# A Fourier-domain block MLP on one Trainium2 core: the first unit's weights are loaded from ScalarE's queue and readied later, and a unit's unfolding begins two groups later

## The chip, the cores and the metric

The kernel runs on one core of one Trainium2 chip. The metric is the device time of an execution in microseconds (us). The time before is a median of three executions; beside it stands one profiled execution, from which all rows below are taken.

## The reference

The input x has shape (4, 128, 128, 768), float32. Everything is computed in float32.

```
xf = rfft2(x, axes=(1, 2), norm='ortho')             # 128 x 65 frequencies, 8 blocks of 96 channels
o1r = relu(xr @ w1[0] - xi @ w1[1] + b1[0]);  o1i = relu(xi @ w1[0] + xr @ w1[1] + b1[1])
o2r = o1r @ w2[0] - o1i @ w2[1] + b2[0];      o2i = o1i @ w2[0] + o1r @ w2[1] + b2[1]
o = softshrink(o2, 0.01)                             # per real and imaginary part
out = irfft2(o, s=(128, 128), norm='ortho') + x
```

## The kernel before

**Units and stages.** A unit is one image with one block of 96 channels, so there are 4 x 8 = 32 units, two by two in the buffers `xs[0]` and `xs[1]` (`par` is the buffer, `m` the pair, `n` the unit). For each unit TensorE runs stage A (DFT along one axis, 24 steps of four rows), then the *layers*, then the *inverse* (stages E and F). The layers go over 17 groups of frequencies (`NS` = 17), `s` running from 0 to 18 because three stages are in flight at once: stage B (first matmul), stage C (DFT along the other axis, which is where the ReLU comes), stage D (second matmul). In the inverse, stage E is the inverse DFT along one axis and stage F the one along the other, in 24 chunks.

**Order of TensorE.** Stage A of unit 0 alone; then for every unit: layers, the first two steps of stage A of the next unit, inverse, the other 22 steps of stage A of the next unit, the last two chunks of F. The engines are separate programs that meet in semaphores; nothing reorders them at run time. The loop holds four units; the first unit's layers of TensorE's loop body and the inverse in the bodies of ScalarE and VectorE are where their programs branch back.

**x in and out.** x is loaded in four pieces, by 50 transfers a unit (14 + 12 + 12 + 12). Before stage A the rows are *folded* (sum and difference of mirrored rows). GpSimd does that for all units but the first (`fold`), which VectorE folds at the start of its program (L578 to L590). Before it folds the next unit, GpSimd multiplies a third of the current unit's x by a half (`halve`, L458), as soon as VectorE has set `first_halved` (L663, the end of `forward`). After the inverse VectorE *unfolds* the unit's x, which has become the result: eight steps, `unfold_step`, one in each of the groups s = 0 to 7 of the next unit's layers. Each odd step releases a piece (`unfolded`), and SyncE then stores that piece, and loads the same piece of the unit two further on. After the first piece's stores SyncE also issues the 28 loads of the next weights for that buffer (`load_w`).

**Weights.** `prepare_step` k = 0 to 8 on VectorE readies the weights of a unit: k = 0 waits until all 28 transfers have landed and negates a part of w1, k = 1 negates another, k = 2 to 5 negate parts of w2 (together they set `w_negated`, which stage B of group 0 waits for), k = 6 to 8 split the second bias (`b2_split`, which stage D of group 0 waits for). They stand in the groups s = 8 to 16 of the layers of the unit before; the first unit's nine stand ahead of `forward(0)`.

**Evictions of stage A.** ScalarE and VectorE take turns in copying the steps of stage A from PSUM (`forward`). TensorE's step 6 needs ScalarE's second copy and step 7 VectorE's second copy.

**SyncE at the start.** The DFT matrices, the 50 transfers of unit 0's x, the 28 of its weights, the 50 of unit 1's x, its 28 of weights.

Of the kernel before, what the change touches and what calls it, by code (L numbers as in the profile page):

```python
# [12 lines left out]
IMAGES, SIZE, HIDDEN, BLOCKS = 4, 128, 768, 8  # L13
BLOCK = HIDDEN // BLOCKS
UNITS = IMAGES * BLOCKS
HALF = SIZE // 2
# [40 lines left out]
NP = len(PIECES)  # L57
# [40 lines left out]
def sum_rows(b):  # L98
# [4 lines left out]
    if b == 0:  # L103
# [14 lines left out]
SEGMENTS = [(0, 0, BLOCK, 0, 0), (0, BLOCK, SIZE, 1, 0), (1, 0, HALF, 1, SIZE - BLOCK), (1, HALF, SIZE, 0, 0),  # L118
            (2, 0, BLOCK - HALF, 0, HALF), (2, BLOCK - HALF, SIZE, 1, 0)]

W2_COLUMNS = [tile * 2 * BLOCK for tile, *_ in SEGMENTS]
# [38 lines left out]
def fourier_mlp(nc, x, w1, b1, w2, b2, dft, out):  # L160
    with ExitStack() as ctx:
# [35 lines left out]
        w1_whole = [sb(f"w1_whole{i}", [SIZE, 2, BLOCK]) for i in range(2)]  # L197
# [158 lines left out]
        def evict_views(g):  # L356
# [5 lines left out]
                return U[0:BLOCK, own:own + A_ROWS - 1, j:j + SIZE], U[0:BLOCK, HALF:HALF + 1, 2:SIZE + 2], third  # L362
            return U[0:BLOCK, own:own + A_ROWS, j:j + SIZE], third

        @block.sync
        def _(sp):
            def load_piece(m, par, p):
                for tile, image in transfers(xs[par], pixels(x, m, par), p):
                    sp.dma_start(tile, image).then_inc(x_loaded[par][p], 16)  # L369

            def load_w(m, par):
                blk = (m % PER_IMAGE) * 2 + par

                def put(dst, src):
                    sp.dma_start(dst, src).then_inc(w_loaded[par], 16)

                put(w1_whole[par][0:BLOCK], w1[:, blk].rearrange("r i o -> i r o"))
                for t, lo, rows in ((w1_whole, BLOCK, slice(HALF, BLOCK)), (w1_halved, 0, slice(0, HALF)),
                                    (w1_halved, HALF, slice(0, HALF))):
                    for half in range(2):  # L380
                        put(t[par][lo:lo + rows.stop - rows.start, half], w1[half ^ 1, blk, rows])
                for (tile, lo, hi, r, c), col in zip(SEGMENTS, W2_COLUMNS):
                    rows = slice(c, c + hi - lo)
                    for half in range(2):

                        put(w2t[par][lo:hi, col + half * BLOCK:col + (half + 1) * BLOCK], w2[half ^ r, blk, rows])
                    with nc.allow_non_contiguous_dma(reason="a bias on each partition"):
                        put(b1t[par][lo:hi, tile:tile + 1], b1[r, blk, rows].unsqueeze(1))
                put(b2_rows[par][:, :, :], b2[:, blk].partition_broadcast(SIZE))
                for row in (0, LOW_ROW):  # L390
                    put(b2t[par][row:row + 1, :].rearrange("p (r c) -> p r c", r=2), b2[:, blk].unsqueeze(0))

            def store_piece(m, par, p):
                sp.wait_ge(unfolded, (m * 2 + par) * NP + (p + 1))
                for tile, image in transfers(xs[par], pixels(out, m, par), p):
                    sp.dma_start(image, tile).then_inc(x_stored[par][p], 16)

            sp.dma_start(mats[:, :], dft[:, 0:7 * SIZE]).then_inc(mats_loaded, 16)
            sp.dma_start(excess[:, :, :].rearrange("p a b -> p (a b)")[:, 0:2 * SIZE],
                         dft[:, 7 * SIZE:]).then_inc(iw_loaded, 16)  # L400
            for p in range(NP):
                load_piece(0, 0, p)
            load_w(0, 0)
            for p in range(NP):
                load_piece(0, 1, p)
            load_w(0, 1)
            with sp.Fori(0, PAIRS - 1) as m:
                for par in range(2):

                    for p in range(NP + 1):  # L410
                        if p < NP:
                            store_piece(m, par, p)
                        if p > 0:
                            sp.wait_ge(x_stored[par][p - 1], (m + 1) * (16 * TRANSFERS[p - 1]))
                            load_piece(m + 1, par, p - 1)
                        if p == 0:
                            load_w(m + 1, par)
            for par in range(2):
                for p in range(NP):
                    store_piece(PAIRS - 1, par, p)  # L420
            for par in range(2):
                for p in range(NP):
                    sp.wait_ge(x_stored[par][p], PAIRS * (16 * TRANSFERS[p]))
# [50 lines left out]
        def _(act):  # L474
# [28 lines left out]
            def forward(n):  # L503
                for at in A_ACT:
                    act.wait_ge(a_done, n * NA + (at + 1))
                    src = bank_a(at).rearrange("p (s j) -> p s j", s=A_ROWS)
                    rows, third = evict_views(A_ORDER[at])
                    act.activation(rows, src[0:BLOCK], ACT.Copy)
                    act.activation(third, src[BLOCK:], ACT.Copy).then_inc(act_copied, 1)
# [38 lines left out]
            def body(loop, unit, last=False):  # L548
# [3 lines left out]
                forward(n)  # L552
                layers(m, par, n)

            forward(0)
            layers(0, 0, 0)
            with act.Fori(0, PAIRS // UNROLL - 1) as loop:
# [7 lines left out]
        def _(dve):  # L565
# [28 lines left out]
            def unfold_step(n, par, k):  # L594

                x_unit, (lo, hi) = xs[par], PIECES[k // 2]
                up, down = x_unit[:, lo:hi + 1, :], mirrored(x_unit, lo, hi)
                if k == 0:
                    dve.wait_ge(f_added, n * NF + NF)
                    dve.wait_ge(f_late_added, n * LATE + LATE)  # L600

                even, odd = x_unit[:, 0, BLOCK:], x_unit[:, MIDDLE, BLOCK:]
                if k % 2 == 0:
                    if k == 0:
                        dve.tensor_tensor(even, even, odd, ALU.add)
                    dve.tensor_tensor(up, up, down, ALU.add).then_inc(unfold_even, 1)
                else:
                    dve.wait_ge(unfold_even, n * NP + (k // 2 + 1))
                    if k == 1:
                        dve.scalar_tensor_tensor(odd, odd, -2.0, even, op0=ALU.mult, op1=ALU.add)  # L610
                    dve.scalar_tensor_tensor(down, down, -2.0, up, op0=ALU.mult, op1=ALU.add).then_inc(unfolded, 1)
# [52 lines left out]
            def layers(m, par, n, first, last):  # L664
                for s in range(NS + 2):
                    if s < NS:
                        k = pairs(s)
                        dve.wait_ge(b_done, n * NS + (s + 1))
                        dve.tensor_copy(mixed[s % 2][:, 0:k], both_b(s)[:, 0:k]).then_inc(b_copied, 1)  # L669
                    for stage in ("sums", "tiles") if s < NS else ("tiles", "sums"):  # L670
                        if stage == "sums" and s >= 2:
                            t, rows = s - 2, rows_d(s - 2)
                            j = 2 + 2 * GROUPS[t][0]
                            dst = real_kw[:, :, :] if t == REAL else U[:, 0:BLOCK, j:j + rows]
                            dve.wait_ge(excess_done, n * NS + (t + 1))
                            dve.scalar_tensor_tensor(dst, parts_d(t), LAMBDA, excess[:, :, 0:rows], op0=ALU.add,  # L676
                                                     op1=ALU.min).then_inc(shrunk, 1)
                        if stage == "tiles" and 1 <= s <= NS:
                            t = s - 1
                            dve.wait_ge(c_done, n * NS + (t + 1))  # L680
                            dve.tensor_scalar(middle[t % 2][:, 0:pairs(t)], middle_c[:, 0:pairs(t)], b1t[par][:, 1:2], 0.0,
                                              ALU.add, ALU.max).then_inc(middle_done, 1)
                    if 2 <= s < NS:

                        k = rows_d(s) // 2
                        dve.wait_ge(shrunk, n * NS + (s - 1))
                        dve.tensor_copy(bank_d(s).rearrange("p (k r) c -> p k r c", r=2)[:, 0:k],  # L687
                                        b2_rows[par][:, :, :].unsqueeze(1).broadcast_to([SIZE, k, 2, BLOCK])).then_inc(seeded, 1)

                    if s < 2 * NP and not first:  # L690
                        unfold_step(n - 1, 1 - par, s)

                    if 2 * NP <= s < 2 * NP + PREPARE and not last:
                        prepare_step(m + par, 1 - par, s - 2 * NP)
            def add(par, n, q):

                x_unit = xs[par]
# [30 lines left out]
                layers(m, par, n, False, last)  # L728


            for k in range(PREPARE):
                prepare_step(0, 0, k)
            forward(0)
            layers(0, 0, 0, True, False)
            with dve.Fori(0, PAIRS // UNROLL - 1) as loop:
                for unit in range(2 * UNROLL):
# [210 lines left out]
```

## Time and profile before

| | us |
|---|---|
| median of 3 executions | 5112.62 (5111.63 to 5113.49) |
| profiled execution, its own time | 5110.49 |
| its span, first to last instruction | 5108.7 |
| TensorE busy | 4994.3 (98%) |
| VectorE busy | 3881.6 (76%) |
| ScalarE busy | 2996.4 (59%) |
| GpSimd busy | 1437.3 (28%) |
| mean granted TensorE clock | 0.994 |

A granted clock of 1.0 is 2.4 GHz and one of 0.5 is 1.2 GHz. PE is TensorE's matmuls, PEld its weight loads, DVE VectorE, ACT ScalarE, POOL GpSimd, SPq SyncE's queue. A float32 matmul of the code is two in the trace. Times in the trace count from the span's start. Stage B of unit 0 begins at 72.48 us, and an undisturbed unit takes 156.56 us from there to the next.

### The profile page before, as it was taken

What the parts mean: (1) busy time and instruction counts of PE and PEld (TensorE: products, weight loads), DVE (VectorE), ACT (ScalarE), POOL (GpSimd) and SP (SyncE); (2) the same over time, 40 slices, a digit from 0 to 9 for tenths busy, and PEclk for the clock granted to TensorE, in tenths of its full rate; (3) what the DMA queues carried; (4) which work ended last, traced back from release to release, by engine and by line L of the source; (5) the groups of instructions that cost most, each with busy time, mean ns of one, the idle gap of its engine ahead of it and who ended that gap; (6) DMA issues with size and microseconds to landing.
All of it is one profiled execution on the core that took longest, in us unless ns stands there. A gap on an engine that the chain in (4) does not pass through costs nothing.

```text
span 5108.7 us, 113601 instructions
## 1 busy us (share of the span) xinstructions
PE 4994.3 (98%) x40128; PEld 4694.0 (92%) x40128; DVE 3881.6 (76%) x6163; ACT 2996.4 (59%) x5409; POOL 1437.3 (28%) x905
## 2 busy tenths in 40 slices
PE   6999999999999999999999999999999999999997
PEld 5999999999999999999999999999999999999996
DVE  4777778777777777777778777788777787777885
ACT  4555665556655566555566555665556655556653
POOL 3033222333123332233331233312333223333120
PEclk8999999999999999999999999999999999999998
DMA  5044422344323444234443234432344422344332
GB/s 113 16 90 105 105 66 57 88 105 105 82 58 83 93 105 102 56 68 90 105 105 68 61 82 105 105 85 62 77 92 105 105 57 65 89 105 105 80 68 57
DMA packets 1699974, 430.34 MB, mean 84 GB/s; under 512 B 1699104, under 2 KB 1699232, under 8 KB 1699360
## 3 DMA queue, kind: packets, MB, share of 16 engines
q1 hardware_dynamic: 1699360, 422.47, 37.4%
q8 instruction: 346, 5.67, 0.5%
q14 instruction: 268, 2.20, 0.1%
HBM read 220.89 MB, written 201.33 MB: 83 GB/s over the span
## 4 chain that ended last, share of the span: by engine, by line
PE 96%; DVE 2%; SPq 1%; issue 1%; ACT 0%; DMA 0%; ACTq 0%; DVEq 0%
PE psum L816 15%; PE psum L787 14%; PE psum L769 13%; PE psum L866 13%; PE psum L839 13%; PE psum L849 9%; PE psum L799 7%; PE psum L876 3%; PE psum L877 3%; PE psum L878 3%; DVE mixed L669 1%; SPq L369 1%; DVE spectrum L647 0%; PE psum L834 0%; PE psum L857 0%
## 5 line engine op out<-in xcount | busy, mean ns | idle before, releaser
L669 DVE COPY mixed<-psum 128x768 f32<-128x768 f32 (+1 forms) x544 | 507.8, 933 | 707.0 <-PE psum L799 705.2
L546 ACT ACTIVATE sums_high<-psum 128x512 fp32r<-128x512 f32 x768 | 459.6, 599 | 730.9 <-PE psum L866 730.9
L816 PEld LDWEIGHTS psum<-mats,mixed 128*128 128x128 f32 x6272 | 744.0, 191 | 121.2 <-issue 113.0
L816 PE MATMUL psum<-mats,mixed 128*128 128x128 f32 x6272 | 841.8, 283 | 0.0
L787 PE MATMUL psum<-w_whole,whole 128*128 128x192 f32 x4160 | 779.3, 329 | 33.0 <-ACT whole L487 13.3
L839 PE MATMUL psum<-w2t,hidden 128*128 128x192 f32 x4160 | 768.2, 327 | 0.0
L769 PE MATMUL psum<-mats,x 128*128 128x128 f32 x6144 | 704.7, 277 | 44.6 <-DVE spectrum L647 28.8
L866 PE MATMUL psum<-mats,spectrum 128*128 128x128 f32 x6144 | 745.1, 275 | 1.7 <-DVE spectrum L676 1.7
L769 PEld LDWEIGHTS psum<-mats,x 128*128 128x128 f32 x6144 | 696.0, 193 | 51.7 <-DVE spectrum L647 29.0
L710 DVE TENSOR_TENSOR sums_low<-psum,sums_high 128x512 fp32r<-128x512 f32 x768 | 531.2, 692 | 247.6 <-ACT sums_high L546 247.3
L787 PEld LDWEIGHTS psum<-w_whole,whole 128*128 128x128 f32 x4160 | 670.9, 196 | 52.2 <-issue 22.9
L866 PEld LDWEIGHTS psum<-mats,spectrum 128*128 128x128 f32 x6144 | 716.2, 192 | 2.4 <-DVE spectrum L676 1.9
L529 ACT ACTIVATE excess<-psum,over 128x768 f32<-128x768 f32 (+1 forms) x544 | 481.8, 886 | 370.3 <-PE psum L849 367.9
L839 PEld LDWEIGHTS psum<-w2t,hidden 128*128 128x128 f32 x4160 | 688.1, 190 | 7.2 <-issue 7.2
L458 POOL TENSOR_TENSOR x<-x,half 128x3072 f32<-128x3072 f32 x32 | 169.8, 5307 | 1730.8 <-DVE halved L663 1730.8
L535 ACT ACTIVATE hidden<-psum,b1t 128x256 f32<-128x256 f32 (+1 forms) x544 | 254.6, 468 | 666.8 <-PE psum L816 666.8
L676 DVE SCALAR_TENSOR_TENSOR spectrum<-psum,excess 128x768 f32<-128x768 f32 (+1 forms) x512 | 481.0, 940 | 109.0 <-ACT excess L529 104.1
L849 PE MATMUL psum<-w2t,middle 64*128 64x192 f32 x4160 | 490.3, 350 | 0.0
L876 PE MATMUL psum<-sums_high,iw_high 128*128 128x260 f32 (+1 forms) x1536 | 461.8, 301 | 0.0
L687 DVE COPY psum<-b_rows 128x768 f32<-128x768 f32 (+1 forms) x480 | 449.9, 937 | 0.0
L450 POOL TENSOR_TENSOR x<-x,doubled 128x640 f32<-128x640 f32 (+1 forms) x248 | 442.7, 1785 | 17.0
L445 POOL TENSOR_TENSOR x<-x 128x640 f32<-128x640 f32 (+1 forms) x248 | 443.8, 1790 | 0.0
(83 smaller groups left out, 7526.3 us busy)
## 6 DMA issues: line engine op xcount, KB each, us to landing
x<-x SPq DMA_DIRECT2D x736, 192.0 KB, 2.9
out<-x SPq DMA_DIRECT2D x736, 192.0 KB, 2.5
x<-x SPq DMA_DIRECT2D x736, 64.0 KB, 2.6
out<-x SPq DMA_DIRECT2D x736, 64.0 KB, 2.2
x<-x SPq DMA_DIRECT2D x32, 144.0 KB, 2.6
w2t<-L_conv_w SPq DMA_DIRECT2D x128, 36.0 KB
out<-x SPq DMA_DIRECT2D x32, 144.0 KB, 2.3
x<-x SPq DMA_DIRECT2D x64, 48.0 KB, 2.3
```

Of the source, the lines that this page charges most:

```text
L529: act.activation(excess[:, :, 0:rows_d(t)], parts_d(t), ACT.Relu, bias=over[:, 0:1]).then_inc(excess_done, 1)
L546: act.activation(sums_high[:, q % RING], bank_e(q), ACT.Copy).then_inc(high_copied, 1)
L669: dve.tensor_copy(mixed[s % 2][:, 0:k], both_b(s)[:, 0:k]).then_inc(b_copied, 1)
L676: dve.scalar_tensor_tensor(dst, parts_d(t), LAMBDA, excess[:, :, 0:rows], op0=ALU.add, op1=ALU.min).then_inc(shrunk, 1)
L710: dve.tensor_tensor(sums_low[:, q % RING], bank_e(q), sums_high[:, q % RING], ALU.subtract).then_inc(low_copied, 1)
L769: last = pe.matmul(bank_a(at)[:, i * SIZE:(i + 1) * SIZE], xs[par][:, j, :], mat(FW_EVEN if g[0] < NP else FW_ODD), start=True, stop=True)
L787: pe.matmul(bank_b(s, k), whole[s % 2][:, k // 2, :, k % 2], w1_whole[par][:, :, :].rearrange("p r o -> p (r o)"), start=k % 2 == 0, stop= ...
L816: last = pe.matmul(out[tile], flat[:, tile * SIZE:(tile + 1) * SIZE], mat(FH), start=True, stop=True)
L839: pe.matmul(sums_d(s, k), hidden[s % 2][:, k // 2, k % 2], w2_tile(par, slice(0, SIZE), 2 * (k // 2)), start=False, stop=False, skip_group ...
L849: last = pe.matmul(sums_d(s, i + 2 * y), middle[s % 2][rows, i], w2_tile(par, rows, 1), start=False, stop=True, skip_group_check=True)
L866: last = pe.matmul(bank_e(q)[:, :, i], U[:, q * CHUNK + i, 4:], mat(IH_FIRST if q * CHUNK < THIRD else IH), start=True, stop=True)
L876: pe.matmul(out, iw_high[:, j], high, start=True, stop=False)
```

## The change

`load_w` becomes a function that takes the engine. The first unit's 28 weight transfers are issued from ScalarE's queue, at the head of its program, and no longer from SyncE's between the two units' x. On VectorE `forward(0)` goes ahead of the first unit's nine `prepare_step`s. In the layers the unfolding stands in the groups 2 to 9 and the preparing in 10 to 18, where they stood in 0 to 7 and 8 to 16.

```diff
+        def load_w(engine, m, par):              # body as before, with engine.dma_start
         @block.sync
...
             for p in range(NP):
                 load_piece(0, 0, p)
-            load_w(0, 0)
             for p in range(NP):
                 load_piece(0, 1, p)
-            load_w(0, 1)
+            load_w(sp, 0, 1)
...
         @block.scalar
+            load_w(act, 0, 0)
             forward(0)
             layers(0, 0, 0)
...
         @block.vector
-                    if s < 2 * NP and not first:
-                        unfold_step(n - 1, 1 - par, s)
-                    if 2 * NP <= s < 2 * NP + PREPARE and not last:
-                        prepare_step(m + par, 1 - par, s - 2 * NP)
+                    if 2 <= s < 2 + 2 * NP and not first:
+                        unfold_step(n - 1, 1 - par, s - 2)
+                    if 2 + 2 * NP <= s < 2 + 2 * NP + PREPARE and not last:
+                        prepare_step(m + par, 1 - par, s - 2 - 2 * NP)
...
+            forward(0)
             for k in range(PREPARE):
                 prepare_step(0, 0, k)
-            forward(0)
             layers(0, 0, 0, True, False)
```

## Rows read from the trace of the kernel before

**Rows 1.** Waits of TensorE, whole span: us in total, times, longest.
```profile
PE psum L769 <- DVE spectrum L647: 28.8, 1, 28.8
...
PE psum L787 <- ACT whole L487: 13.3, 26, 1.9
PE psum L787 <- ACT whole L480: 11.3, 6, 2.1
...
PE psum L866 <- DVE spectrum L676: 1.7, 1, 1.7
```
**Rows 2.** Timeline of the start: start, length, instruction, idle before.
```profile
1.67 28.95 SPq L369 DMA_DIRECT2D x<-x  x50
...
36.41 0.16 DVE L592 MEMSET spectrum<- 96x126 f32 x1
...
45.15 1.36 SPq L375 DMA_DIRECT2D b2t<-L_conv_b  x2
...
47.80 0.21 DVE L620 TENSOR_SCALAR w_whole<-w_whole 32x96 f32<-32x96 f32 x1 [11.23 <-DMA b2t<-L_conv_b]
...
48.28 0.91 DVE L624 TENSOR_SCALAR w2t<-w2t 32x96 f32<-32x96 f32 x4
...
50.22 0.17 DVE L637 MEMSET spectrum<- 96x130 f32 x1
...
53.18 17.38 PE L769 MATMUL psum<-mats,x 128*128 128x128 f32 x136 [28.84 <-DVE spectrum L647]
```
**Rows 3.** Windows: length, busy (count) per engine, granted clock, DMA share, GB/s.
```profile
12.00:31.00 19.00, 8.60 (x58) 8.43 (x58) 10.60 (x9) 4.75 (x8) 0.00 (x0) 0.88 1.03 234
...
249.00:266.00 17.00, 17.00 (x138) 15.67 (x134) 14.22 (x15) 11.62 (x22) 0.00 (x0) 1.00 0.19 36
...
53.20:57.20 4.00, 4.00 (x19) 4.00 (x20) 2.71 (x4) 0.20 (x1) 0.00 (x0) 0.50 0.90 190
57.30:70.50 13.20, 13.20 (x119) 13.06 (x117) 10.10 (x20) 9.34 (x17) 0.00 (x0) 1.00 1.01 210
```
**Rows 4.** Timeline, end of unit 0's stage A and begin of its layers.
```profile
72.48 1.58 PE L787 MATMUL psum<-w_whole,whole 128*128 128x192 f32 x8 [1.92 <-ACT whole L487]
72.57 0.22 DVE L663 COPY halved<-spectrum 64x66 f32<-64x66 f32 x1
72.94 5.31 POOL L458 TENSOR_TENSOR x<-x,half 128x3072 f32<-128x3072 f32 x1 [72.10 <-DVE halved L663]
...
80.29 1.54 POOL L445 TENSOR_TENSOR x<-x 128x640 f32<-128x640 f32 x1
```
**Rows 5.** Timeline, VectorE instructions that overlap one of GpSimd in unit 1.
```profile
229.44 5.31 POOL L458 TENSOR_TENSOR x<-x,half 128x3072 f32<-128x3072 f32 x1 [109.01 <-DVE halved L663]
...
232.40 2.40 DVE L605 TENSOR_TENSOR x<-x 128x32 f32<-128x32 f32 x1
...
308.75 1.82 POOL L450 TENSOR_TENSOR x<-x,doubled 128x768 f32<-128x768 f32 x1
308.99 1.70 DVE L626 CAST b_parts<-b2t 1x192 fp32r<-1x192 f32 x1
```
**Rows 6.** Windows of the same columns: unit 0 (no unfolding), unit 1 (unfolding).
```profile
72.40:228.90 156.50, 155.87 (x1254) 146.50 (x1254) 100.92 (x178) 93.45 (x171) 46.12 (x29) 1.00 0.06 12
229.00:385.50 156.50, 155.86 (x1254) 146.50 (x1254) 120.11 (x193) 93.51 (x170) 46.11 (x29) 1.00 0.39 86
```
**Rows 7.** Timeline of unit 1: unfolding, store, the last fold stretch, the layers' end.
```profile
239.20 9.06 SPq L396 DMA_DIRECT2D out<-x  x14
...
246.57 1.75 DVE L611 SCALAR_TENSOR_TENSOR x<-x 128x1536 f32<-128x1536 f32 x1
...
315.04 1.47 POOL L444 TENSOR_TENSOR doubled<-x 128x768 f32<-128x768 f32 x1 [4.47 <-DMA x<-x]
...
325.80 0.76 DVE L676 SCALAR_TENSOR_TENSOR spectrum<-psum,excess 128x576 f32<-128x576 f32 x1 [0.92 <-ACT excess L529]
...
326.99 3.74 PE L866 MATMUL psum<-mats,spectrum 128*128 128x128 f32 x32
```

More of the change, by code:

```diff
@@ L363, in evict_views, with put @@
             return U[0:BLOCK, own:own + A_ROWS, j:j + SIZE], third
+        def load_w(engine, m, par):
+            blk = (m % PER_IMAGE) * 2 + par
+            def put(dst, src):
+                engine.dma_start(dst, src).then_inc(w_loaded[par], 16)
+            put(w1_whole[par][0:BLOCK], w1[:, blk].rearrange("r i o -> i r o"))
+            for t, lo, rows in ((w1_whole, BLOCK, slice(HALF, BLOCK)), (w1_halved, 0, slice(0, HALF)),
+                                (w1_halved, HALF, slice(0, HALF))):
+                for half in range(2):
+                    put(t[par][lo:lo + rows.stop - rows.start, half], w1[half ^ 1, blk, rows])
+            for (tile, lo, hi, r, c), col in zip(SEGMENTS, W2_COLUMNS):
+                rows = slice(c, c + hi - lo)
+                for half in range(2):
+                    put(w2t[par][lo:hi, col + half * BLOCK:col + (half + 1) * BLOCK], w2[half ^ r, blk, rows])
+                with nc.allow_non_contiguous_dma(reason="a bias on each partition"):
+                    put(b1t[par][lo:hi, tile:tile + 1], b1[r, blk, rows].unsqueeze(1))
+            put(b2_rows[par][:, :, :], b2[:, blk].partition_broadcast(SIZE))
+            for row in (0, LOW_ROW):
+                put(b2t[par][row:row + 1, :].rearrange("p (r c) -> p r c", r=2), b2[:, blk].unsqueeze(0))
         @block.sync
@@ L369, in load_piece @@
                     sp.dma_start(tile, image).then_inc(x_loaded[par][p], 16)
[L371 to L391, printed above, removed]
             def store_piece(m, par, p):
@@ L416, in _ @@
                         if p == 0:
-                            load_w(m + 1, par)
+                            load_w(sp, m + 1, par)
             for par in range(2):
```

## The prediction

> **What bounds the kernel now.** The busy table says 98% for TensorE, so I read its waits first, then the places where they stand. Over the whole span TensorE waits for little: once 28.8 us in the first unit's stage A for VectorE's copies, 13.3 us in 26 units for ScalarE's first gather, 11.3 us in six units for a later gather (only where the loop branches back), and once for VectorE's last shrink [rows 1]. The only large stall is the first. The timeline of the start shows what is behind it: VectorE has done its last folding and its memset at 36.41 + 0.16 = 36.57, then stands idle for 11.23 us until the last weight transfer lands, readies the weights in nine short steps from 47.80, and comes to the first instruction of `forward(0)` at 50.22; TensorE, which needs the second copy of that function, goes on at 53.18 [rows 2]. The weights are late because their 28 issues stand in SyncE's queue behind 50 of x, which take until 1.67 + 28.95 = 30.62 [rows 2].
>
> The windows of unit 0 and unit 1 answer the other half. Unit 0 has no unfolding and unit 1 has it; in 156.50 us TensorE has 1254 matmuls and 155.87 and 155.86 us of busy time [rows 6]. VectorE's 19 us more of work cost TensorE nothing, so moving the unfolding to other groups has nothing to win; it can only lose.
>
> **The first stall.** With the wait for the weights gone from ahead of `forward(0)`, its first instruction follows at 36.57 and no longer at 50.22: **-13.65 us**, if x lands when it did. ScalarE's 28 issues last about what SyncE's did, 45.15 + 1.36 - 30.62 = 15.9 us [rows 2], so ScalarE is free for its evictions near 18 us; its first four are wanted only when VectorE's second is there, around 40. That is cover of 20 us, and it costs nothing. SyncE's queue, freed of the 28, brings unit 1's x and weights some 13 us earlier; nobody waits for them yet.
>
> The weights now share the 16 DMA engines with x. In unit 1 the same 28 transfers are alone in the queue and take 0.19 of 17.0 us, 3.2 us of all engines [rows 3]. From 12 to 31 us the share under x alone is 1.03 [rows 3], so there is no room and the last piece of x lands later by the weights' work: **+3.0 us**. The bounds are 0 (the work fits into gaps) and 15.9 (every issue of ScalarE holds up one of SyncE); I stay near the row of the work, as the engines are what is full.
>
> On the last point the Trainium skill has a rule. Perfetto Trace Analysis, in its section on the HWDGE DMA instruction, draws one descriptor generator that two sequencers share, with a wait for its lock. By it the term would be up to 15.9 us and not 3.0. No row here has two queues issuing at once.
>
> **What the nine steps cost in their new place.** They stand between `forward(0)` and the layers now, and stage B of group 0 waits for the first six. At their old speed these take 48.28 + 0.91 - 47.80 = 1.39 us [rows 2]; after L663, which ends at 72.79, that would put stage B at 74.2 where it was 72.48 [rows 4] (I keep the clock of before for this part; all of it comes earlier together). But L663 also releases GpSimd's halving, 5.31 us from 72.94 [rows 4], and the two engines exclude one another in such operations. L605, a 32-element operation, took 2.40 us and ended when GpSimd's L458 did (229.44 + 5.31 = 234.75); L626, on one partition, took 1.70 us and ended with GpSimd's L450 [rows 5]. So: step 0 slips in and ends at 73.03; the halving runs to 78.34; step 1 follows; GpSimd now goes on to fold unit 1, whose x has landed by then, and steps 2 to 5 each get in between two of its four short operations, which fill the 2.04 us from the halving's end at 78.25 to L445 at 80.29 [rows 4]. The sixth step ends near 80.4 and stage B begins near 80.5: **+8.0 us**. The lower bound is 1.8 (the six go through in one burst), the upper 10 (each meets a long fold step). Steps 6 to 8 lie beside stage B of group 0, and cost nothing.
>
> TensorE is then idle for 10 us from 70.56 (53.18 + 17.38). After its long wait the granted clock was 0.50 from 53.2 to 57.2, and 19 matmuls were done where 13.20 us at 1.00 have 119 [rows 2, 3]: 210 ns each for 111. I count such a stretch once more: 4.0 x (1 - 111/210) = **+1.9 us**.
>
> Start in all: -13.65 + 3.0 + 8.0 + 1.9 = -0.75 us.
>
> **The move by two groups.** The unfolding's second step, which releases the first store at 239.20, now ends where the fourth did: 246.57 + 1.75 less the first piece's smaller size, 248.3. SyncE is busy without a break from there, so stores, loads, and GpSimd's folding are all 9.4 us later. Folding ends near 315.04 + 20 + 9.4 = 345. Its last piece feeds the last six steps of stage A, 48 matmuls at 111 ns and two chunks of F ahead of unit 2's stage B at 385.6 (229.04 + 156.56), so about 378: cover of 30 us remains. Unfolding ends before folding starts, as before.
>
> Preparing now reaches into the end of the layers. Step 7 stands ahead of VectorE's last shrink, L676 at 325.80, which had 0.92 us of idle time before it and ends 326.99 - 326.56 = 0.43 us before stage E begins [rows 7]. Free of GpSimd, step 7 fits (such a step takes 0.21 us [rows 2]). GpSimd's last unbroken stretch of folding, from 315.04 for 20 us [rows 7], is moved to 324.5, so that it is busy just then in nearly every unit. If step 7 has to wait w for a fold operation and ends with it, as L626 did, TensorE loses w - 0.92 - 0.43 = w - 1.35 us. The fold operations are one of 1.47 and two of 1.82 us in turn [rows 5, 7]; over an arbitrary phase that is (2 x 0.47^2 / 2 + 0.12^2 / 2) / 5.11 = 0.045 us a unit, in 30 units **+1.3 us**. The bounds are 0 (step 7 always falls right) and 0.47 x 30 = 14 (the phase always falls worst). Step 8 comes after the last shrink, with 2 us to the next work of VectorE.
>
> In six units the programs of VectorE and ScalarE branch back just as stage E begins, and the x loads, now 9 to 11 us later, reach into that moment. What the wait for a branch costs beside loads has no row; the nearest is the 11.3 us in six units where TensorE branches [rows 1]. Bounds 0 and 11; I take **+1 us**, since an idle DMA queue did not spare TensorE that wait either.
>
> **Sum.** -0.75 + 1.3 + 1.0 = +1.55 us on the profiled execution's 5110.49, that is 5112.0. The median of the runs, 5112.62, lies 2.1 us above the profiled execution, so 5114.2 for the median. 0.2% of it, 10.2 us, is what a measurement can tell from no change: below 5102.4 is faster, above 5122.8 slower.
>
> **The rivals.**
> *The steps go through in one burst.* For it: the nine ran without a gap when GpSimd was idle [rows 2]. Against it: both rows of an overlap show VectorE wait for GpSimd's whole operation [rows 5]. The sum has 1.8 for 8.0: 5108.0; with nothing for DMA work, clock and move, 5100.8, the only way to the faster side. Chance 0.25. The Trainium skill, SBUF - State Buffer, "Who interferes with whom", says that whichever starts first has the shared ports for its whole instruction; by it this rival is out and the 8.0 stands.
>
> *The issues of the two queues wait for each other.* Then each of ScalarE's 28 puts SyncE's back, the last x lands 15.9 us later, and the stall is not shorter but 2.3 us longer: 5114.2 + 12.9 = 5127.1, slower. It decides from a delay of x of 11.6 us on (3.0 and the 8.6 up to 5122.8). For it: an issue of either kind takes about 0.57 us, whatever its bytes (28.95/50, 15.9/28 [rows 2]), so it isn't the data that sets it. Against it: the DMA share of 1.03 says the engines are the limit. Chance 0.11.
>
> *The phase locks at the worst.* Step 7 meets the begin of a long fold operation in most units: up to 12.7 us more, 5127, slower. Landing times vary by some us between units, which speaks against it. Chance 0.06.
>
> My forecast has the remaining 0.58. Faster gets 0.08, from the first rival's far end; slower gets 0.14, mostly the second and third; the same 0.78. The range reaches from the first rival's lower middle, 5104, to 5122.
>
> **What would show it.** Stage B of unit 0 should begin near 70 us (72.48 - 10.65 + 8.0), with a wait of 10 us ahead of it and VectorE's L620 on `w1_halved` over 5 us long beside L458. TensorE's first wait should be 18 us for 28.8. The last x of unit 0 should land about 3 us later. The stretch from unit to unit should stay 156.56 us in most units, with single ones 0.1 to 0.6 us longer and a wait of E on L676. If stage B of unit 0 begins at 64, the lock was wrong; if above 80, the queues block each other.

## The result, and the profile after

The changed kernel takes 5119.27 us (median of 11 runs) where the kernel before takes 5111.61 (11 runs beside it): ratio 1.0018, 95% interval 1.0010 to 1.0026, so 7.7 us more by the medians; the interval is 0.10 to 0.26%. The forecast was 5114.2, which is +1.6 us on its own base. The direction and the range hold; four fifths of the size were not in the sum. Of all runs here and below one counts as slow and is left out of its ratio: 5677 us, in the experiment in which GpSimd waits. The profiled execution's span is 5116.5 us against 5108.7, +7.8, nearly the difference of the medians, so that its rows can be added up.

First the waits of TensorE in the changed kernel, over the whole span (us in total, times, longest); lines have moved by one against [rows 1].

```profile
PE psum L770 <- DVE x L591: 17.5, 2, 16.5
PE psum L770 <- DVE spectrum L648: 15.8, 1, 15.8
PE psum L788 <- ACT whole L486: 11.4, 25, 0.6
PE psum L788 <- ACT whole L479: 11.3, 6, 2.2
PE psum L788 <- DVE w2t L625: 10.2, 1, 10.2
...
PE psum L867 <- DVE sums_low L711: 2.4, 4, 1.2
PE psum L867 <- DVE spectrum L677: 1.7, 1, 1.7
```

The reader is to see three things. The wait of 28.8 us is now 15.8; of these 13.0 us the start gained only 11.2, as the waits for the first folded pieces of x (L591, 17.5 us where they were 15.7 before, a wait that the prediction did not list) grew by 1.8. A wait of 10.2 us for L625, the negating of w2, has come. And stage E (L867) waits for VectorE's low sums, four times, which it never did for more than 0.1 us before (the view counts no wait under 0.15 us; two more of 0.11 and 0.12 are there).

The timeline of the start, to be held against [rows 2] and [rows 4]:

```profile
1.66 61.20 SPq L391 DMA_DIRECT2D x<-x  x100
...
15.04 1.82 ACTq L369 DMA_DIRECT2D b2t<-L_conv_b  x2
...
35.28 1.76 DVE L587 TENSOR_TENSOR x<-x 128x1536 f32<-128x1536 f32 x1 [3.21 <-DMA x<-x]
...
39.01 0.17 DVE L638 MEMSET spectrum<- 96x130 f32 x1
...
41.97 17.96 PE L770 MATMUL psum<-mats,x 128*128 128x128 f32 x136 [15.84 <-DVE spectrum L648]
...
61.95 0.22 DVE L664 COPY halved<-spectrum 64x66 f32<-64x66 f32 x1
62.20 0.21 DVE L621 TENSOR_SCALAR w_whole<-w_whole 32x96 f32<-32x96 f32 x1
62.32 5.30 POOL L457 TENSOR_TENSOR x<-x,half 128x3072 f32<-128x3072 f32 x1 [61.48 <-DVE halved L664]
...
62.44 5.25 DVE L621 TENSOR_SCALAR w_halved<-w_halved 128x96 f32<-128x96 f32 x1
...
67.72 2.08 DVE L625 TENSOR_SCALAR w2t<-w2t 32x96 f32<-32x96 f32 x4
...
70.13 2.92 PE L788 MATMUL psum<-w_whole,whole 128*128 128x192 f32 x8 [10.20 <-DVE w2t L625]
```

`forward(0)` begins at 39.01 for 50.22, 11.2 us earlier. Stage A ends 10.6 us earlier (41.97 + 17.96 = 59.93 for 70.56). Stage B begins 2.35 us earlier (70.13 for 72.48): 8.3 us are lost between these two. The second L621, on `w_halved`, takes 0.21 us when alone (in the run in which GpSimd waits, below) and here ends with GpSimd's L457.

Windows around stage B of unit 0, and around the begin of unit 16 (columns as in [rows 3]):

```profile
70.20:74.50 4.30, 4.30 (x16) 3.49 (x16) 3.01 (x3) 0.00 (x0) 4.14 (x4) 0.50 0.12 25
74.60:80.00 5.40, 5.40 (x38) 4.96 (x37) 2.00 (x3) 4.60 (x9) 5.18 (x5) 1.00 0.24 32
...
2586.80:2590.10 3.30, 3.30 (x15) 2.42 (x14) 0.08 (x1) 0.08 (x1) 3.30 (x1) 0.50 0.00 0
2590.20:2594.00 3.80, 3.80 (x28) 3.36 (x27) 1.82 (x3) 2.97 (x7) 0.00 (x0) 1.00 0.00 0
```

The first line of each pair is a stretch at 0.50 of the clock. After the first of them unit 1's stage B begins at 228.76, where it was at 229.04: at that point all that the start gives is 0.28 us.

```profile
228.76 0.93 PE L788 MATMUL psum<-w_whole,whole 128*128 128x192 f32 x4 [0.43 <-ACT whole L486]
```

The rest of the time is read from the distances of the stage-B begins from unit to unit, after less before:

| where | us |
|---|---|
| begin of unit 0's stage B | -2.35 |
| unit 0 | +2.07 |
| the six units in which VectorE and ScalarE branch back (4, 8, ... 24) | +6.63 |
| the six units that end in TensorE's branch | +0.15 |
| the other 18 | +1.02 |
| the last | +0.32 |

Together that is 7.8 us, the difference of the spans. So the layers of an ordinary unit cost nearly nothing, and the six branching units carry the loss. Here is the worst, unit 8, at the begin of its stage E, first in the changed kernel:

```profile
1423.28 1.82 POOL L444 TENSOR_TENSOR x<-x 128x768 f32<-128x768 f32 x1
1423.91 1.31 DVE L629 CAST b_high<-b2t 1x192 fp32r<-1x192 f32 x1
...
1425.25 0.76 DVE L677 SCALAR_TENSOR_TENSOR spectrum<-psum,excess 128x576 f32<-128x576 f32 x1
...
1426.04 1.17 DVE L632 TENSOR_TENSOR b_parts<-b2t,b_high 1x192 fp32r<-1x192 f32 x1
...
1429.50 1.89 DVE L711 TENSOR_TENSOR sums_low<-psum,sums_high 128x512 fp32r<-128x512 f32 x3 [2.29 <-ACT sums_high L545]
1430.25 0.94 PE L867 MATMUL psum<-mats,spectrum 128*128 128x128 f32 x6 [1.24 <-DVE sums_low L711]
```

and in the kernel before:

```profile
1424.71 0.76 DVE L676 SCALAR_TENSOR_TENSOR spectrum<-psum,excess 128x576 f32<-128x576 f32 x1 [0.92 <-ACT excess L529]
...
1427.98 1.29 DVE L710 TENSOR_TENSOR sums_low<-psum,sums_high 128x512 fp32r<-128x512 f32 x2 [2.51 <-ACT sums_high L546]
```

After the last shrink VectorE needs 2.51 us to its first low sum in the kernel before, though ScalarE's high sum, which the column names, was there at 1427.60: in between lies the branch back of VectorE's program. In the changed kernel it is 3.49 us from the end of the shrink (1426.01 to 1429.50), and TensorE, whose fourth chunk of stage E waits for it, stands for 1.24 us. Two things are new in the place: L632 of the preparing, lengthened by GpSimd, and x in the queues (GpSimd is busy for 5.84 of 6 us in both). The windows from 1424 to 1430, before and after (the columns as above, the last two the DMA share and GB/s):

```profile
1424.00:1430.00 6.00, 6.00 (x53) 5.83 (x53) 2.63 (x4) 2.95 (x6) 5.84 (x5) 1.00 0.03 8
```

```profile
1424.00:1430.00 6.00, 5.00 (x42) 4.69 (x42) 3.64 (x4) 2.96 (x5) 5.84 (x4) 1.00 0.83 164
```

Which of the two delays VectorE was the question of the first experiments.

### The profile page after: what moved, and what is told of

Its sections match the earlier page's. It is cut to its first block, busy times and chain, and to the rows that moved or that the text cites. A ratio compares the mean times of both kernels' runs of the same rounds, so it can differ in the third digit from the quotient of the medians.

```text
span 5116.5 us, 113601 instructions
## 1 busy us (share of the span) xinstructions
PE 5002.0 (98%) x40128; PEld 4698.7 (92%) x40128; DVE 3828.6 (75%) x6163; ACT 2995.7 (59%) x5409; POOL 1437.1 (28%) x905
## 4 chain that ended last, share of the span: by engine, by line
PE 95%; DVE 2%; issue 1%; SPq 1%; ACT 0%; DMA 0%; DVEq 0%; ACTq 0%
PE psum L817 15%; PE psum L788 14%; PE psum L770 13%; PE psum L840 13%; PE psum L867 13%; PE psum L850 9%; PE psum L800 7%; PE psum L877 3%; PE psum L878 3%; PE psum L879 3%; DVE mixed L670 1%; SPq L391 1%; DVE spectrum L648 0%; PE psum L835 0%; PE psum L858 0%
## 5 line engine op out<-in xcount | busy, mean ns | idle before, releaser
L867 PE MATMUL psum<-mats,spectrum 128*128 128x128 f32 x6144 | 746.8, 275 | 4.4 <-DVE sums_low L711 2.4
L770 PE MATMUL psum<-mats,x 128*128 128x128 f32 x6144 | 705.5, 277 | 33.3 <-DVE x L591 17.5
L867 PEld LDWEIGHTS psum<-mats,spectrum 128*128 128x128 f32 x6144 | 716.2, 192 | 6.6 <-DVE sums_low L711 3.8
L457 POOL TENSOR_TENSOR x<-x,half 128x3072 f32<-128x3072 f32 x32 | 169.8, 5306 | 1428.0 <-DVE halved L664 1428.0
L440 POOL TENSOR_TENSOR x<-x 128x192 f32<-128x192 f32 x31 | 15.7, 506 | 1739.3 <-DMA x<-x 1739.3
```

The source lines that it names most:

```text
L770: last = pe.matmul(bank_a(at)[:, i * SIZE:(i + 1) * SIZE], xs[par][:, j, :], mat(FW_EVEN if g[0] < NP else FW_ODD), start=True, stop=True)
L867: last = pe.matmul(bank_e(q)[:, :, i], U[:, q * CHUNK + i, 4:], mat(IH_FIRST if q * CHUNK < THIRD else IH), start=True, stop=True)
```

## The experiments

Each was run beside the kernel before on the same chip. The ratios are to it, with their 95% intervals; a difference in us is of the medians.

**The two halves of the change.** First the start alone (layers as before):

```diff
-                    if 2 <= s < 2 + 2 * NP and not first:
-                        unfold_step(n - 1, 1 - par, s - 2)
+                    if s < 2 * NP and not first:
+                        unfold_step(n - 1, 1 - par, s)
...
-                    if 2 + 2 * NP <= s < 2 + 2 * NP + PREPARE and not last:
-                        prepare_step(m + par, 1 - par, s - 2 - 2 * NP)
+                    if 2 * NP <= s < 2 * NP + PREPARE and not last:
+                        prepare_step(m + par, 1 - par, s - 2 * NP)
```

> Only the start of the change: ScalarE issues the first weights, the nine steps stand behind the first stage A; the layers are as before. My theory (the start wins 13 us of waiting and gives it all back to GpSimd's halving and a low clock): stage B of unit 0 again near 70.1 us with a 10 us wait ahead of it, the time within 1.5 us of before (-0.3 us by the profile of the changed kernel), and every later unit as before. Rival (the start itself costs what was measured, by a clock or DMA effect that lasts): +4 us or more.

Measured: 5110.80 against 5111.40, ratio 0.9999 (0.9990 to 1.0008). The waits:

```profile
PE psum L770 <- DVE spectrum L648: 15.6, 1, 15.6
...
PE psum L788 <- DVE w2t L625: 10.2, 1, 10.2
```

The start is worth -0.6 us, and 0 lies within the interval. My theory holds; no effect of it that lasts is seen.

Then the move by two groups alone, put into the kernel before (the same lines the other way round, and nothing else).

> Only the move by two groups, unfolding in groups 2 to 9 and preparing in 10 to 18; the start is as before. My theory: it carries the whole loss, +7 to +8.5 us. Waits of stage E on VectorE's low sums in the six units where the programs branch back, 2 to 4 us in all, and about 1.3 us of late last shrinks. Rival: the loss sits in the start, and this run is within 2 us of before.

Measured: 5122.30 against 5111.40, ratio 1.0020 (1.0011 to 1.0029), +10.9 us, more than I expected; its interval overlaps that of the whole change nearly in full. The move carries the loss.

```profile
PE psum L866 <- DVE sums_low L710: 4.1, 6, 1.1
PE psum L866 <- DVE spectrum L676: 3.0, 7, 1.6
```

The second row holds the last unit's 1.6 us, which every kernel here has; the other 1.4 us are six late last shrinks.

**The two halves of the move.** Preparing alone in groups 10 to 18, with unfolding, stores and loads where they were:

```diff
-                    if 2 * NP <= s < 2 * NP + PREPARE and not last:
-                        prepare_step(m + par, 1 - par, s - 2 * NP)
+                    if 2 + 2 * NP <= s < 2 + 2 * NP + PREPARE and not last:
+                        prepare_step(m + par, 1 - par, s - 2 - 2 * NP)
```

> Unfolding in groups 0 to 7 as before, so stores, loads and GpSimd's folding at their old times; only preparing moved to groups 10 to 18. Theory A (preparing's last two steps, which wait for GpSimd's fold operations, stand ahead of the last shrink and ahead of VectorE's branch): the loss is here without any load beside it, +3 to +6 us, VectorE's first low sum 1 us or more late in the branching units. Theory B (the x loads, moved into the moment of the branch, slow the fetch of the programs): the branching units are as before, the run is at +1.5 us at most, from the late shrinks alone.

Measured: 5115.73 against 5111.40, ratio 1.0010 (1.0001 to 1.0019), +4.3 us.

```profile
PE psum L866 <- DVE spectrum L676: 3.1, 6, 1.7
PE psum L866 <- DVE sums_low L710: 0.5, 2, 0.2
```

The time is as theory A says, but not where it says it: the low sums are waited for only twice, 0.5 us in all (and three times for 0.10 to 0.15 us, which the view leaves out). In unit 8 of this run the first low sum starts 1.15 us after L631 ends (1428.53 + 1.17 = 1429.70 to 1430.85), 2.35 us after the end of the shrink, which is less than before (2.51). So VectorE's branch does not wait for step 8 in full. What is late is the last shrink, behind step 7; stage E begins later for it in eleven units, by 0.67 us at most. In unit 8 (L628 is step 7, L631 step 8) the shrink follows step 7 at once, though ScalarE's part of it had been there for 0.43 us:

```profile
1426.45 1.26 DVE L628 CAST b_high<-b2t 1x192 fp32r<-1x192 f32 x1
1427.74 0.76 DVE L676 SCALAR_TENSOR_TENSOR spectrum<-psum,excess 128x576 f32<-128x576 f32 x1
1428.53 1.17 DVE L631 TENSOR_TENSOR b_parts<-b2t,b_high 1x192 fp32r<-1x192 f32 x1
1430.85 2.01 DVE L710 TENSOR_TENSOR sums_low<-psum,sums_high 128x512 fp32r<-128x512 f32 x3 [1.15 <-ACT sums_high L546]
```

Then the unfolding two groups later, so with the loads at their new times, but the preparing packed so that none of it is left for the groups 17 and 18:

```diff
-                    if s < 2 * NP and not first:
-                        unfold_step(n - 1, 1 - par, s)
+                    if 2 <= s < 2 + 2 * NP and not first:
+                        unfold_step(n - 1, 1 - par, s - 2)
...
-                    if 2 * NP <= s < 2 * NP + PREPARE and not last:
-                        prepare_step(m + par, 1 - par, s - 2 * NP)
+                    if 2 + 2 * NP <= s < NS and not last:
+                        lo = (0, 2)[s - 2 - 2 * NP] if s - 2 - 2 * NP < 2 else s - 2 * NP
+                        for k in range(lo, lo + (2 if s - 2 - 2 * NP < 2 else 1)):
+                            prepare_step(m + par, 1 - par, k)
```

> Unfolding in groups 2 to 9, loads 9.4 us later as in the change; the nine preparing steps packed into groups 10 to 16 (two in each of the first two), so that none is left for groups 17 and 18. Theory A (the last two preparing steps): within 1 us of before, no wait of stage E beyond 0.1 us. Theory B (the loads beside the branch): +3 to +6 us, with VectorE's first low sum late in the branching units though nothing stands ahead of the branch.

Measured: 5115.41 against 5111.40, ratio 1.0008 (0.9999 to 1.0017), +4.0 us, as theory B says.

```profile
PE psum L868 <- DVE sums_low L712: 3.2, 6, 1.1
PE psum L868 <- DVE spectrum L676: 1.7, 1, 1.7
```

No late shrink is left beside the last unit's, and the waits for low sums are all there, in all six branching units. In unit 8:

```profile
1424.24 0.76 DVE L676 SCALAR_TENSOR_TENSOR spectrum<-psum,excess 128x576 f32<-128x576 f32 x1 [0.92 <-ACT excess L529]
1428.45 1.89 DVE L712 TENSOR_TENSOR sums_low<-psum,sums_high 128x512 fp32r<-128x512 f32 x3 [3.45 <-ACT sums_high L546]
```

3.45 us from the shrink to the first low sum with nothing between them but the branch, where it was 2.51; the DMA share of the moment is 0.78 (1423.50 to 1429.50) and was 0.03. In the six branching units this distance is 2.72 to 3.61 us and was 2.27 to 2.59. That a program is fetched there can be seen in the DMA queues. From 1424.80 to 1428.00 of the kernel before they carry four packets of the kind `instruction` and nothing else; in this run, from 1424.30 to 1428.50 (packets, MB, share of the engines):

```profile
q1 hardware_dynamic: 3069, 0.75, 86.4%
q14 instruction: 4, 0.03, 2.5%
q8 instruction: 1, 0.02, 1.4%
```

The instruction packets themselves are no longer than before (those of 8 KB take 0.3 to 0.6 us in both, a single one 0.7), but the first of them comes 1.20 to 1.88 us after ScalarE's branch in the six units, where it was 0.86 to 1.10. So the fetch gets under way later beside the loads; what holds it back the trace doesn't say. GpSimd's folding moved with the loads and is a rival of them, but it is busy for 5.84 of 6 us at this place in both kernels; no run moves one without the other.

Both theories are right for about 4 us each by the medians: step 7 for the shrinks, the loads for the branches. (The interval of this run just reaches 1, and 4.3 + 4.0 falls short of the 10.9 of the move by what such intervals allow; that the two add up exactly isn't shown.)

**Do the loads cost only where they meet a branch?** The last kernel again, and the kernel before, each with eight units in the loop's body, so with two branches back and not six:

```diff
-        UNROLL = 2
+        UNROLL = 4
```

> Unfolding two groups later with the preparing packed ahead of group 17 (start of before), and eight units in the loop's body: two branches and not six, the loads still 9.4 us later. If the loads cost only where they meet a branch, TensorE waits for low sums twice, 1.1 us in all where it was 3.2, and the run is at +1.3 us against the kernel of before with eight units in its body. If they cost anywhere: +4 us as with six branches.

> The kernel of before with eight units in the loop's body, the base for the other run: four branches fewer at 1.3 to 1.6 us each, -5.3 us against before.

Measured: 5105.89 for the packed one (ratio to before 0.9990, 0.9981 to 0.9999) and 5103.48 for the base (0.9987, 0.9978 to 0.9996); before 5110.57. The packed one's waits:

```profile
PE psum L868 <- DVE spectrum L676: 1.7, 1, 1.7
PE psum L868 <- DVE sums_low L712: 1.1, 2, 0.6
```

Two waits for low sums, 1.1 us in all, where there were six and 3.2; the base has none. So they belong to the branches. The difference of the medians, +2.4 us, lies between the +1.3 and the +4 expected, and the intervals of the two ratios overlap: by the time alone this would not be settled, by the waits it is. The four units that no longer branch say the same: their first low sum comes 2.16 us after the shrink at a DMA share of 0.7 to 1.0 as it does in the base at 0.0, and GpSimd folds beside them, too. The base is 7.1 us faster than before where I expected 5.3.

**The start: is it the halving?** As the start alone, with GpSimd's first halving held back until all nine steps are done:

```diff
+            pool.wait_ge(b2_split, 3)
             halve(0, 0)
```

> The start of the change alone, with one wait more: GpSimd's halving of the first unit waits until all nine preparing steps are done, so nothing of GpSimd runs beside them. If the shared access of VectorE and GpSimd is what costs 8 us there: L620 on w1_halved takes 0.2 us and not 5.25, the wait ahead of stage B of unit 0 falls from 10.2 to about 4 us, stage B begins near 64 us, the time is 6 us below before (8 if the clock does not fall in the shorter wait). If the wait has another cause: still 10 us, and no change.

Measured: 5103.54 against 5111.53, ratio 0.9984 (0.9975 to 0.9994), -8.0 us; against the start alone 7.4 us.

```profile
62.21 0.21 DVE L622 TENSOR_SCALAR w_halved<-w_halved 128x96 f32<-128x96 f32 x1
62.45 0.91 DVE L626 TENSOR_SCALAR w2t<-w2t 32x96 f32<-32x96 f32 x4
...
63.69 2.92 PE L789 MATMUL psum<-w_whole,whole 128*128 128x192 f32 x8 [3.98 <-DVE w2t L626]
...
64.44 5.31 POOL L457 TENSOR_TENSOR x<-x,half 128x3072 f32<-128x3072 f32 x1 [63.60 <-DVE b_parts L633]
```

The same instruction takes 0.21 us where it took 5.25, the next four 0.91 where they took 2.08, and the wait is 3.98 where it was 10.20. The wait of GpSimd is the only edit to the start alone, which has the changed kernel's numbers here (5.25, 2.08, 10.2), so this is shown and not argued.

**The start without the detour.** ScalarE issues the weights and VectorE's order stays as before:

```diff
-            forward(0)
             for k in range(PREPARE):
                 prepare_step(0, 0, k)
+            forward(0)
             layers(0, 0, 0, True, False)
```

> Only the issue from ScalarE; the nine preparing steps stay ahead of the first stage A, the layers are as before. The steps run at 39 to 41.4 us with GpSimd idle, forward(0) begins at 41.4 for 50.22, stage B of unit 0 at 63.7 for 72.48 with no wait of note ahead of it: -8.8 us. Rival (ScalarE's queue costs x more than 3 us, or another stall takes the place): -5 us or less.

Measured: 5102.41 against 5111.53, ratio 0.9982 (0.9973 to 0.9991), -9.1 us. `forward(0)` begins at 41.60, stage B of unit 0 at 63.44.

Then the nine steps ahead of the last piece's folding, where VectorE waits for x (the definition of `prepare_step` moves up for it):

```diff
             for i, (lo, hi) in enumerate(PIECES):
+                if i == NP - 1:
+                    for k in range(PREPARE):
+                        prepare_step(0, 0, k)
...
-            for k in range(PREPARE):
-                prepare_step(0, 0, k)
             forward(0)
```

> As the run with ScalarE's issue alone, but the nine preparing steps stand ahead of the last piece's folding, in 3.2 us in which VectorE waits for x anyway: another 2.4 us, so -11.2 us against before; forward(0) begins at 39.0 and stage B of unit 0 at 61.3.

Measured: 5100.41 against 5111.53, ratio 0.9978 (0.9969 to 0.9987), -11.1 us.

```profile
31.78 0.21 DVE L586 TENSOR_SCALAR w_whole<-w_whole 32x96 f32<-32x96 f32 x1
...
33.76 0.35 DVE L597 TENSOR_TENSOR b_parts<-b2t,b_high 1x192 fp32r<-1x192 f32 x1
35.09 1.76 DVE L612 TENSOR_TENSOR x<-x 128x1536 f32<-128x1536 f32 x1 [0.98 <-DMA x<-x]
```

The nine steps lie in a wait of which 0.98 us is left: they cost nothing.

**Both together.** The last kernel with eight units in the loop's body.

> As the run before it, with eight units in the loop's body and not four, so that each program branches back twice and not six times. If a branch costs TensorE 1.3 to 1.6 us over an ordinary unit, -11.2 - 4 x 1.5 = -17 us; TensorE's long waits at the layers' begin two and not six. Rival (the wait is for the fetch of straight code, wherever it stands): no more than -11.2.

Measured: 5095.07 (6 runs) against 5111.53, ratio 0.9968 (0.9956 to 0.9980), -16.5 us. TensorE's long waits at the layers' begin:

```profile
PE psum L789 <- ACT whole L479: 3.9, 2, 2.1
```

Two, 3.9 us, for six and 11.3 [rows 1]. This is the fastest version.

## Why the prediction was right in direction and short in size

**The start, four terms.** Each was sized within 1 us, and the sum, -0.75, came out at -0.28: here mechanism and size were right.
- *x later by 3.0 us.* The last piece's folding begins at 35.28 for 32.81, 2.5 us; `forward(0)` is 11.2 us early where I had 10.65. ScalarE's 28 issues ended at 16.9 us, while SyncE went on at 0.61 us an issue (61.20/100) for 0.58. The rival in which each issue of one queue puts back one of the other is out: 28 issues beside SyncE's put x back by 2.5 us and not by 15.9. With it goes, as a cost of that size, the wait for the shared descriptor generator of Perfetto Trace Analysis, "DMA Instruction - HWDGE", in the Trainium skill. Whether the 2.5 us are the engines' work or come from the issuing isn't shown: SyncE's own first 50 issues end 2.4 us later (33.0 for 30.6).
- *The steps against GpSimd, +8.0.* Measured +8.3, in the order forecast: step 0 slips in, step 1 waits out the halving, the other four alternate with the fold operations. The rival of one burst is out, and the run that holds GpSimd back shows the cause.
- *The clock, +1.9.* 16 matmuls in 4.30 us at 0.50, and unit 0 is 2.07 us longer.
- Not in the sum: stage A itself took 17.96 us for 17.38, 0.6 us. With it: -11.21 + 0.58 + 8.28 + 2.07 = -0.28 us.

**"The unfolding has nothing to win."** Right: the 18 plain units are 1.02 us longer in all, none shorter by more than 0.03.

**Step 7 ahead of the last shrink, +1.3.** The mechanism was right and so was the size in the profile of the changed kernel: 1.0 us over the 18 plain units. Stage E begins late for it in six units, by 0.26 us at most (unit 9). With the preparing alone moved it was more (+4.3 us by the medians, 3.6 us over the 18 plain units of its profile), perhaps because the phase of GpSimd's folding is another there; that was not tried by itself. The rival with the phase locked at the worst is out: it did not reach 14 us in any run.

**The term that failed: "+1 us" for the loads beside the branch.** I had written that an idle DMA queue did not spare TensorE its wait for a branch, and took from it that a full one would not add to VectorE's. It does. The waits for low sums alone are 2.4 us in the changed kernel, 3.2 with the preparing out of the way, and the six branching units are together 6.6 us longer, 3.5 of it without the two stretches of the next paragraph. The way to see it was open: in the kernel before, VectorE's low sum came 2.27 to 2.59 us after its last shrink in the branching units and 2.16 us after it in the others, so the branch stood there as a wait that had used up what TensorE's fourth chunk leaves (0.05 us of wait in unit 12), and the move put 0.8 of DMA share on top of it. I gave the term a bound of 11 and the wrong value within it.

**What no step had: single stretches at half clock.** In units 16 and 24, behind TensorE's own branch waits of 2.09 and 2.20 us, the granted clock was 0.50 for 3.4 us, and stage E began 1.56 and 1.52 us late, 3.1 of the 6.6. In the profile before, waits up to 2.10 us had no such stretch behind them. Nine of the ten profiles of experiments have one or two of them within the loop, faster kernels among them (in the start alone it is unit 12, 1.6 us longer than before, with the other five branching units within 0.3), so I don't count them to the change; whether it makes them more frequent stays open. The spread of the changed kernel's runs (5117.86 to 5128.94, before 5109.99 to 5113.49) would fit that.

The sum by the profile: -0.3 (start) + 3.1 (half clock in two units) + 3.5 (the rest of the branching units, 2.4 of it waits for low sums) + 1.0 (late shrinks) + 0.5 (the last unit and TensorE's branches) = +7.8 us. So 4.5 us of it, the branching units' and the shrinks', go back to the move, as its halves show, and 3.1 are not shown to come from the change at all.

That the time lies within the range is partly luck. No sum of the prediction stands behind the range's upper end, 5122, and the two things that made most of the loss, 3.5 and 3.1 us, stood in the sum with 1 us together.

## What to carry to other kernels

A wait that is removed from the head of a program is worth only what the moved work costs in its new place: here nine steps of 2.3 us cost nothing inside a wait for x, 2.0 us more ahead of the first copy (5102.41 against 5100.41, the intervals overlap), and 8 us where GpSimd is released at the same moment. Before moving small VectorE operations on SBUF, look at what GpSimd does then; each can cost a whole GpSimd operation (5.25 us here). And work that only shifts transfers in time isn't free because its queue has slack: look where the loop branches back, for there the program is fetched by transfers too, and that took longer beside others.

## What the runs showed of the hardware that was not expected

- Over a branch back VectorE needed 2.51 us from its last instruction to its next with the DMA engines' share at 0.03, and 3.45 us with it at 0.78 (unit 8; 2.27 to 2.59 and 2.72 to 3.61 over the six units).
- VectorE's short operations don't pass GpSimd's in a group: four that take 0.91 us alone took 2.08 us beside the first four operations of GpSimd's fold, one of which got in behind each.
- Eight units for four in the loop's body (two branches back for six) gave 7.1 us of 5111 in a kernel whose TensorE is 98% busy, and 5.3 us on top of the better start.
- Waits of TensorE of about 2 us were sometimes followed by 3.4 us at half the clock and sometimes not (2.09 us with it in the changed kernel, 2.10 without it before; over all profiles 1.77 us with it in the run with the steps in the folding, unit 8, and 2.20 without it in the run in which GpSimd waits, unit 16).
